# Graph attention layers on one core: value projections moved five slots back, weights and first slots in another order

## Chip, cores and metric

One core of a Trainium2 chip. The metric is the device time of one execution in microseconds; lower is better.

## What is computed

128 graphs of 128 nodes with 512 features, one adjacency matrix `adj` for all. Two layers, each behind a layer norm without weights (`h` is always the normalised, rectified x):

```python
h = relu(layernorm(x));  a = adj @ h              # per graph
x = x + relu(max_over_features(a) + b0)           # what the reference's first layer comes to
q, k, v = h2 @ Wq + bq, h2 @ Wk + bk, h2 @ Wv + bv   # 8 heads of 64
x = x + softmax(q k^T / 8, masked by adj == 0) @ v
```

The column added by the first layer is the same for all features of a node, so the second layer norm gives the same h as the first (but for eps); the kernel uses one h for both. `bv` is added to x at the end, as the weights of a softmax sum to 1.

## The kernel before

The work goes by graphs, one slot per graph, with an instruction order written out by hand for each engine and semaphores between them. Products are made at about float32 precision from float16 pairs: each operand is a head (the float16 value) and a rest (what the head lacks), and three matmuls (head x head, head x rest, rest x head) stand for one (PAIRS). Each matrix is scaled by a power of two found from its largest absolute value (`peak_of`, `peak_to_rows` on TensorE, `scales_of`), then `w_head` (ScalarE, L378) and `w_rest` (VectorE, L525) split it.

In a slot k, by engine:

- TensorE: scores of graph k-5 (L660); two chunks of the q/k projection of the group of four graphs that k lies in (L631, 12 matmuls of 512 columns each; chunks 0 to 3 are q, 4 to 7 k); the adjacency product of graph k+4 (L616, three matmuls); the values of graph k (`v_rows`, L643, 12 matmuls); probabilities times values of graph k-6 (`probs_times_v`, L675).
- ScalarE: the head of the values of k-1 (`v_head`, L343), the column c of k, the two normalising passes of k+5 (L324, L325), both q/k outputs (`qk_out`, L336 and L338), both exp passes of k-5 (L353, L355), x + c of k (`add_c`, L373, into `xc`).
- VectorE: the maximum of the adjacency product of k+3 (`adjacency_out`, L434), the rest of the values of k-1 (`v_rest`, L439), the softmax shift of k-5 (L450, L454, L457), the output of k-7 (`attention_out`, L464 to L473), the moments of k+6.
- GpSimd: the rest of h of k+5 (L263), rests of q/k (L280), scales of the norm, the rest of the probabilities (L287), x + bv (`add_bv`, L272).
- SP issues all large DMAs: the load of k+7, the transposes of h of k+5 (L193, into `hT`, two groups of four graphs) and of the probabilities of k-5 (L201), the store of k-7. A chunk with u = 0 waits for the transposes of all four graphs of its group.

PSUM: one bank for the adjacency product, one for the values, two for q/k chunks, two for scores, two for probabilities times values (`o_ps`, one graph at a time). So the values of the next graph wait for `v_evac` of the one before, its adjacency for `a_evac`, its outputs for `y_done`.

Before the slots, the first four graphs are normalised, multiplied by the adjacency and transposed, and the weights come in order q, v, k (`MATRICES`), each in one DMA of 1 MB; the k weights are split within slot 0. After the last slot, `TAIL` works off scores, softmax and outputs of the last five graphs, with three sets of banks for the scores (`TAIL_BANKS`).

## Time and profile before

| | us |
|---|---|
| median of 3 runs | 1354.16 (1354.02 to 1355.4) |
| the profiled execution: its time | 1353.57 |
| its span (first to last instruction) | 1351.7 |
| TensorE busy with matmuls | 1298.4 (96%) |
| VectorE busy | 1069.5 (79%) |
| ScalarE busy | 943.1 (70%) |
| GpSimd busy | 1103.6 (82%) |

The span is divided by the timeline into a start, 123 like slots, and an end. A busy share says how much an engine had to do on average, not what set the end; the chain of waits does that. Matmuls that follow each other overlap in the records, so their pace is read from start to start. TensorE's granted clock has two levels here, 1.2 and 2.4 GHz (0.50 and 1.00 in a window).

### The profile page before, as it was taken

How to read it: one execution, taken by the hardware profiler on the slowest of the kernel's cores; microseconds unless marked ns; L12 is line 12 of the kernel's file. 1: busy time of each engine (PE TensorE's matmuls, PEld its weight loads, DVE VectorE, ACT ScalarE, POOL GpSimd, SP SyncE). 2: the span in 40 equal slices, each digit the busy share in tenths (PEclk: the TensorE clock that was granted, in tenths of full speed). 3: DMA queues.
4: the chain of work that ended last, by engine and by line, in shares of the span. 5: the costliest groups of instructions: out<-in, count | busy, mean ns of one | idle time of the engine just before them, and what ended most of it. 6: DMA issues, size and time to landing. Idle time of an engine off the chain costs nothing.

```text
span 1351.7 us, 30371 instructions
## 1 busy us (share of the span) xinstructions
PE 1298.4 (96%) x11145; PEld 681.7 (50%) x11145; DVE 1069.5 (79%) x2229; ACT 943.1 (70%) x1422; POOL 1103.6 (82%) x1160
## 2 busy tenths in 40 slices
PE   4899999999999999999999999999999999999983
PEld 1345555555555555555555555555555555555542
DVE  6458788788887887878878878878788788788777
ACT  4667777777677677677777776777767777767552
POOL 2678898898888888888888888898888898888652
PEclk9999999999999999999999999999999999999995
DMA  7245566565565565665665656656656566566445
GB/s 204 48 91 123 132 133 135 124 141 134 120 141 132 127 138 128 133 141 120 135 138 126 134 132 133 135 127 137 136 119 141 132 133 132 128 140 126 93 73 132
DMA packets 441491, 173.22 MB, mean 128 GB/s; under 512 B 406784, under 2 KB 406912, under 8 KB 441344
## 3 DMA queue, kind: packets, MB, share of 16 engines
q1 hardware_dynamic: 440000, 171.03, 58.0%
q8 instruction: 88, 1.44, 0.4%
q14 instruction: 59, 0.48, 0.1%
q10 hardware_dynamic: 1344, 0.27, 0.1%
HBM read 37.03 MB, written 33.55 MB: 52 GB/s over the span
## 4 chain that ended last, share of the span: by engine, by line
PE 94%; DVE 2%; ACT 0%; DMA 0%; issue 0%; POOLq 0%; ACTq 0%; DVEq 0%
PE proj L631 49%; PE proj L643 24%; PE sc L660 7%; PE o_ps L675 7%; PE proj L616 6%; DVE y L473 1%; DVE masked L450 0%; DVE row_max L454 0%; DVE shifted L457 0%; DMA probsT<-probs 0%; DVE w L525 0%; POOLq L38 0%; ACT qkT L336 0%; ACT qk L338 0%; DVE out_scale L467 0%
## 5 line engine op out<-in xcount | busy, mean ns | idle before, releaser
L631 PE MATMUL proj<-hT,w 128*128 128x512 f16 x3072 | 688.5, 381 | 9.5 <-DMA hT<-h 5.1
L631 PEld LDWEIGHTS proj<-hT,w 128*128 128x128 f16 x3072 | 291.0, 98 | 358.7 <-issue 14.8
L643 PE MATMUL proj<-w,hT 128*128 128x512 f16 x1536 | 352.4, 379 | 1.1 <-DVE w L525 1.1
L336 ACT ACTIVATE qkT<-proj,bqk_up 128x512 f16<-128x512 f32 x256 | 173.5, 678 | 247.2 <-PE proj L631 247.2
L280 POOL TENSOR_TENSOR qkT<-qk,qkT 128x512 f16<-128x512 f32 x256 | 310.8, 1214 | 29.7 <-ACT qk L338 29.3
L287 POOL TENSOR_TENSOR probs<-probs 128x1024 f16<-128x1024 f32 x128 | 273.1, 2134 | 24.3 <-ACT probs L355 24.3
L263 POOL TENSOR_TENSOR h<-h 128x512 f16<-128x512 f32 x125 | 236.1, 1889 | 11.7 <-ACT h L324 8.3
L643 PEld LDWEIGHTS proj<-w,hT 128*128 128x128 f16 x1536 | 150.2, 98 | 182.5 <-DVE w L525 1.5
L439 DVE SCALAR_TENSOR_TENSOR v<-proj,v 128x512 f16<-128x512 f32 x128 | 88.5, 692 | 190.0 <-ACT v L343 190.0
L473 DVE SCALAR_TENSOR_TENSOR y<-o_ps,out_scale,x 128x64 f32<-128x64 f32 x1024 | 208.3, 277 | 4.6
L457 DVE TENSOR_TENSOR shifted<-masked,row_max 128x1024 f32<-128x1024 f32 x128 | 207.9, 1624 | 4.4
L450 DVE SCALAR_TENSOR_TENSOR masked<-sc,score_scale,mask 128x1024 f32<-128x1024 f32 x125 | 160.4, 1283 | 32.4 <-PE sc L660 32.3
L353 ACT ACTIVATE probs<-shifted 128x1024 f16<-128x1024 f32 x128 | 135.3, 1057 | 67.5 <-DVE shifted L457 65.5
L338 ACT ACTIVATE qk<-proj,bqk_up 128x512 f32<-128x512 f32 x256 | 173.8, 679 | 0.0
L272 POOL TENSOR_TENSOR x<-xc,bv_rows 128x512 f32<-128x512 f32 x128 | 163.1, 1274 | 0.0
L454 DVE TENSOR_REDUCE row_max<-masked 128x8 f32<-128x1024 f32 x128 | 156.2, 1220 | 4.4
L242 POOL TENSOR_TENSOR var_eps<-mean_var,eps 128x1 f32<-128x1 f32 x128 | 24.7, 193 | 141.1 <-DVE mean_var L426 141.1
L675 PEld LDWEIGHTS o_ps<-v,probsT 128*128 128x128 f16 x3072 | 113.8, 99 | 48.8 <-DMA probsT<-probs 15.2
L675 PE MATMUL o_ps<-v,probsT 128*128 128x65 f16 (+1 forms) x3072 | 118.1, 195 | 18.9 <-DMA probsT<-probs 14.5
L355 ACT ACTIVATE probs<-shifted 128x1024 f32<-128x1024 f32 x128 | 133.2, 1041 | 0.0
L343 ACT ACTIVATE v<-proj 128x512 f16<-128x512 f32 x128 | 76.4, 597 | 57.8 <-PE proj L643 57.5
L324 ACT ACTIVATE h<-x_in,h_add,h_mul 128x512 f32<-128x512 f32 x128 | 102.8, 803 | 13.0 <-POOL h_add L252 13.0
(59 smaller groups left out, 999.1 us busy)
## 6 DMA issues: line engine op xcount, KB each, us to landing
x_in<-in_x SPq DMA_DIRECT2D x128, 256.0 KB, 3.5
out_x<-y SPq DMA_DIRECT2D x128, 256.0 KB, 2.3
hT<-h SPq DMA_TRANSPOSE x128, 3.0
probsT<-probs SPq DMA_TRANSPOSE x128, 4.3
w_raw<-in_L_gnn_Wq SPq DMA_DIRECT2D x1, 1024.0 KB, 8.9
w_raw<-in_L_gnn_Wv SPq DMA_DIRECT2D x1, 1024.0 KB, 11.1
w_raw<-in_L_gnn_Wk SPq DMA_DIRECT2D x1, 1024.0 KB, 12.8
bv_rows<-in_L_gnn_bv ACTq DMA_DIRECT2D x1, 256.0 KB, 6.6
```

The source lines that it names most:

```text
L263: pool.tensor_tensor(h16[:, k % 4, 1, :], h32[:, k % 2, :], h16[:, k % 4, 0, :], ALU.subtract).then_inc(h_rest_done, 1)
L272: pool.tensor_tensor(x1[:, k % RING, :], xc[:, k % 2, :], bv_rows[:, :], ALU.add).then_inc(x1_done, 1)
L280: pool.tensor_tensor(qk_place(k, u, 1), qk32[:, u % 2, :], qk_place(k, u, 0), ALU.subtract).then_inc(qk_rest_done, 1)
L287: pool.tensor_tensor(probs16[:, k % 2, 1, :, :], probs[:, :, :], probs16[:, k % 2, 0, :, :], ALU.subtract).then_inc(probs_rest_done, 1)
L336: nc.scalar.activation(qk_place(k, u, 0), place, ACT.Identity, scale=P_SCALE, bias=bias).then_inc(qk_head_done, 1)
L338: nc.scalar.activation(qk32[:, u % 2, :], place, ACT.Identity, scale=P_SCALE, bias=bias).then_inc(qk_evac, 1)
L450: nc.vector.scalar_tensor_tensor(masked[:, :, :], banks[:, :, :].rearrange("p t (h n) -> p (t h) n", n=P), score_scale[:, :], mask8[:, :]. ...
L457: nc.vector.tensor_tensor(shifted[:, :, :], masked[:, :, :], row_max[:, :].unsqueeze(2).to_broadcast([P, H, P]), ALU.subtract).then_inc(sh ...
L473: last = nc.vector.scalar_tensor_tensor(y[:, k % 2, cols], o_view[:, h // 4, h % 4, 0:HD], out_scale[:, h // 4, h % 4:h % 4 + 1], x1[:, k ...
L631: last = nc.tensor.matmul(proj[:, u % 2, :], w16[:, j, s, c, col * P:(col + 1) * P], hT[:, k // GROUP % 2, t, c, :, :].rearrange("p g n -> ...
L643: last = nc.tensor.matmul(proj[:, V_BANK, :], hT[:, k // GROUP % 2, s, c, k % GROUP, :], w16[:, 2, t, c, :], start=(c == 0 and i == 0), st ...
L675: last = nc.tensor.matmul(o_view[:, h // 4, h % 4, 0:w], probsT[:, k % 2, s, h % 2 * 4 + h // 2, :], v16[:, t, k // GROUP % 2, k % GROUP, ...
```

## The change

- The values of graph k are projected in slot k+5 (`V_BEHIND` 5), their head and rest follow one slot later (`V_OUT_BEHIND` 6). For that `hT` holds three groups instead of two; `v16` holds one set of four graphs instead of two, so `v_head` also waits for `o_ready` of k-4.
- In the tail, values of the last five graphs stand between their scores; VectorE takes their rests behind the softmax of the same graph, and the outputs of four graphs come at the end. The score banks there are two sets.
- The q weights come in four DMAs with a maximum of each; the order is q, k, v (v behind the x loads). `w_rest` signals each quarter, and chunks 0 and 4 and the first values wait quarter by quarter.
- The first five slots have orders of their own on ScalarE and GpSimd (`early_slot`); k's weights are split in slot 1, v's in slots 3 and 4; graph 4 is normalised in slot 0. The first four transposes are issued by their own loop with semaphores of their own, the others as before.
- `add_c` writes `x1` itself (waiting for `y_done`), `add_bv` adds bv to it in place, four slots later.

```diff
-V_BEHIND, Y_BEHIND = 1, 7
+V_BEHIND, V_OUT_BEHIND, Y_BEHIND, BV_BEHIND = 5, 6, 7, 4
+HT_GROUPS = 3
...
-        hT = sb("hT", [P, 2, 2, KC, GROUP, P], F16)
+        hT = sb("hT", [P, HT_GROUPS, 2, KC, GROUP, P], F16)
...
-        v16 = sb("v16", [P, 2, 2, GROUP, H, VP], F16)
+        v16 = sb("v16", [P, 2, GROUP, H, VP], F16)
...
-        MATRICES = (3, 0, 2, 1)
+        MATRICES = (3, 0, 1, 2)
         TAIL = [(B, k) for k in range(-ATTN_BEHIND, 0)]
-        TAIL_BANKS = (sc, proj[:, 0:2, :], proj[:, 2:4, :])
...
-            for j, w in ((0, wq), (2, wv), (1, wk)):
-                sp.dma_start(w_raw[:, j, :, :], w.rearrange("(c p) n -> p c n", p=P)).then_inc(w_loaded[j], 16)
+            for c in range(KC):
+                sp.dma_start(w_raw[:, 0, c, :], wq[c * P:(c + 1) * P, :]).then_inc(q_loaded[c], 16)
+            sp.dma_start(w_raw[:, 1, :, :], wk.rearrange("(c p) n -> p c n", p=P)).then_inc(w_loaded[1], 16)
             for k in range(PREP_AHEAD, LOAD_AHEAD):
                 load(0, k)
+            sp.dma_start(w_raw[:, 2, :, :], wv.rearrange("(c p) n -> p c n", p=P)).then_inc(w_loaded[2], 16)
...
-                    wait(sp, qk_ready, 2 * (m - m % GROUP - GROUP))
-                    wait(sp, v_ready, m + 1 - 2 * GROUP)
+                    wait(sp, qk_ready, 2 * (m - m % GROUP - (HT_GROUPS - 1) * GROUP))
+                    wait(sp, v_ready, m + 1 - HT_GROUPS * GROUP)
...
-            for k in range(TURN_AHEAD):
-                transpose(0, k)
+            for k in range(GROUP):
+                sp.wait_ge(h_rest_done, k + 1)
+                sp.dma_start_transpose(group_T(k), h16[:, k, :, :].rearrange("p s n -> p (s n)")).then_inc(hT_first[k], 16)
             for k in range(B):
+                if k == 0:
...
-                transpose_probs(B, k)
-                store(B, k - 2)
-            store(B, -2)
-            store(B, -1)
+            for i in range(ATTN_BEHIND):
+                transpose_probs(B, i - ATTN_BEHIND)
+                if i != 2:
+                    store(B, i - STORE_BEHIND - (i > 2))
+            for k in range(-3, 0):
+                store(B, k)
...
+                    pool.tensor_tensor(x1[:, k % RING, :], x1[:, k % RING, :], bv_rows[:, :], ALU.add).then_inc(x1_done, 1)
 
             def qk_rest(base, k, u):
...
-            for k in range(DVE_RESTS, NORM_AHEAD):
+            for k in range(DVE_RESTS, PREP_AHEAD):
...
-                norm_scales(0, k + 1)
+            norm_scales(0, 4)
+            norm_scales(0, 5)
...
+            def early_slot(base, k):
+                u = 2 * (k % GROUP)
+                qk_rest(base, k, u)
+                if k == 0:
+                    rest(base, 4)
+                rest(base, k + NORM_AHEAD)
+                qk_rest(base, k, u + 1)
+                norm_scales(base, k + MOMENTS_AHEAD)
+                add_bv(base, k - BV_BEHIND)
...
                 probs_rest(base, k - ATTN_BEHIND)
                 qk_rest(base, k, u + 1)
-                add_bv(base, k)
-
-            slots(pool, slot)
+                add_bv(base, k - BV_BEHIND)
+
+            for k in range(ATTN_BEHIND):
...
+                slot(0, k)
+            for k in range(-BV_BEHIND, 0):
+                add_bv(B, k)
             for graph in TAIL:
                 probs_rest(*graph)
 
...
+                    nc.scalar.activation(v16[:, 0, k % GROUP, :, 0:HD],
...
                     act.wait_ge(c_done, m + 1)
-                    wait(act, x1_done, m - 1)
-                    nc.scalar.activation(xc[:, k % 2, :], x_in[:, k % RING, :], ACT.Identity, bias=c_col[:, k % RING, :]).then_inc(xc_done, 1)
-
...
-            normalise(0, 4)
-            w_head(2, 2)
             act.wait_ge(bias_loaded, 64)
...
+            def early_slot(base, k):
+                u = 2 * (k % GROUP)
+                if k == 4:
+                    w_head(2, 3)
+                qk_out(base, k, u)
+                if k == 0:
+                    normalise(base, 4)
+                if k == 1:
+                    w_head(1, 2)
+                qk_out(base, k, u + 1)
+                normalise(base, k + NORM_AHEAD)
+                c_of(base, k)
+                add_c(base, k)
...
-                v_head(base, k - 1)
+                v_head(base, k - V_OUT_BEHIND)
...
+            for k in range(ATTN_BEHIND):
+                early_slot(0, k)
+            for k in range(ATTN_BEHIND, B):
+                slot(0, k)
+            v_head(B, -V_OUT_BEHIND)
+            for k in range(-V_BEHIND, 0):
+                v_head(B, k)
+                exps(B, k)
...
+                    nc.vector.scalar_tensor_tensor(w16[:, j, 1, c, :], w_raw[:, j, c, :], up[:, j:j + 1],
+                                                          w16[:, j, 0, c, :], ALU.mult, ALU.subtract).then_inc(rests_done, 1)
...
+            nc.vector.tensor_scalar(mask8[:, :], adj_sb[:, :], 0.0, -8e9, ALU.is_equal, ALU.mult).then_inc(mask_done, 1)
...
+            q_peak_of(0)
             moments(3)
             first_rest(0)
+            q_peak_of(1)
+            first_rest(1)
...
+            q_peak_of(2)
+            q_peak_of(3)
+            dve.wait_ge(q_peaks_done, KC)
+            dve.wait_ge(floor_done, 2)
+            peak_of(0, q_peaks[:, :])
+            floored(0, 2)
             first_rest(2)
-            adjacency_out(0, 1)
...
             scales_of(1)
             projection_scales(0, 1)
             w_rest(0, 1)
+            adjacency_out(0, 0)
             moments(4)
-            w_peak_of(2, 3)
-            adjacency_out(0, 3)
+            moments(5)
+            w_peak_of(1, 3)
+            for k in range(1, PREP_AHEAD):
+                adjacency_out(0, k)
+            moments(6)
             scales_of(2)
-            projection_scales(2, 2)
...
+            projection_scales(1, 2)
+            w_rest(1, 2)
+            dve.wait_ge(undo_done, 2)
+            nc.vector.tensor_tensor(score_scale[:, :], undo[:, 0:1], undo[:, 1:2], ALU.mult).then_inc(score_scale_done, 1)
+            dve.wait_ge(score_scale_done, 1)
             dve.wait_ge(mask_done, 2)
...
-                if base + k > 0:
+                if k > 0:
                     adjacency_out(base, k + AMAX_AHEAD)
-                v_rest(base, k - V_BEHIND)
+                v_rest(base, k - V_OUT_BEHIND)
                 softmax_shift(base, k - ATTN_BEHIND)
...
+                if k > 0:
+                    stats_of(base, k + MOMENTS_AHEAD)
+                    moments_wait(base, k + MOMENTS_AHEAD)
+                    moments_of(base, k + MOMENTS_AHEAD)
+
+            for k in range(B):
+                slot(0, k)
+                if k == 2:
+                    w_peak_of(2, 4)
+                if k == 3:
+                    scales_of(3)
+                    projection_scales(2, 3)
+                    w_rest(2, 3)
+                    dve.wait_ge(redo_done, 3)
+            v_rest(B, -V_OUT_BEHIND)
             for i, graph in enumerate(TAIL):
...
+                softmax_shift(*graph, TAIL_BANKS[i % 2])
+                if i != 2 and i != 4:
+                    attention_out(B, i - Y_BEHIND - (i > 2))
+                v_rest(*graph)
+            for k in range(-4, 0):
                 attention_out(B, k)
...
-                    wait(pe, a_evac, base + k)
+                    wait(pe, a_evac, 1 if k == PREP_AHEAD else base + k)
...
+                        if k < GROUP and col == 0:
+                            pe.wait_ge(rests_done, 2 + j * KC + c)
...
+                        if base + k == 0:
+                            pe.wait_ge(rests_done, 2 + 2 * KC + c)
                         for i, (s, t) in enumerate(PAIRS):
-                            last = nc.tensor.matmul(proj[:, V_BANK, :], hT[:, k // GROUP % 2, s, c, k % GROUP, :],
+                            last = nc.tensor.matmul(proj[:, V_BANK, :], hT[:, (base + k) // GROUP % HT_GROUPS, s, c, k % GROUP, :],
...
+            peak_to_rows(1)
...
-                if isinstance(base, int) and base + k == 0:
+                if k == 1:
                     peak_to_rows(2)
                 qk_chunk(base, k, u + 1)
                 adjacency(base, k + PREP_AHEAD)
+                if k == 3:
+                    peak_to_rows(3)
+                v_rows(base, k - V_BEHIND)
+                probs_times_v(base, k - OUT_BEHIND)
+
+            for k in range(B):
+                slot(0, k)
+            for i, (base, k) in enumerate(TAIL):
+                if i == 1:
+                    pe.wait_ge(qk_evac, 2 * B)
+                if i > 1:
+                    pe.wait_ge(masked_done, base + k - 1)
+                scores(base, k, TAIL_BANKS[i % 2])
                 v_rows(base, k)
-                probs_times_v(base, k - OUT_BEHIND)
-
-            slots(pe, slot, after_first=lambda: peak_to_rows(3))
-            scores(*TAIL[0])
-            pe.wait_ge(qk_evac, 2 * B)
-            scores(*TAIL[1], TAIL_BANKS[1])
-            pe.wait_ge(v_evac, B)
-            scores(*TAIL[2], TAIL_BANKS[2])
-            probs_times_v(B, -OUT_BEHIND)
-            for i, (base, k) in enumerate(TAIL):
-                if i + 3 < len(TAIL):
-                    pe.wait_ge(masked_done, base + k + 1)
-                    scores(*TAIL[i + 3], TAIL_BANKS[i % 3])
-                probs_times_v(base, k)
+                if i == 1 or i == 3:
+                    probs_times_v(B, i // 2 - OUT_BEHIND)
+            for k in range(-4, 0):
+                probs_times_v(B, k)
```

## Rows read from the trace of the kernel before

**Rows 1.** The page: the span, and the chain that ended last by line.

```profile
span 1351.7 us, 30371 instructions
...
PE proj L631 49%; PE proj L643 24%; PE sc L660 7%; PE o_ps L675 7%; PE proj L616 6%; DVE y L473 1%; DVE masked L450 0%; DVE row_max L454 0%; DVE shifted L457 0%; DMA probsT<-probs 0%; DVE w L525 0%; POOLq L38 0%; ACT qkT L336 0%; ACT qk L338 0%; DVE out_scale L467 0%
```

**Rows 2.** TensorE's timeline, first 100 us: start, length, engine, line, work, [idle before, releaser].

```profile
24.42 4.24 PE L631 MATMUL proj<-hT,w 128*128 128x512 f16 x12 [5.08 <-DMA hT<-h]
...
40.60 7.03 PE L631 MATMUL proj<-hT,w 128*128 128x512 f16 x24 [4.45 <-ACT qk L338]
49.43 0.81 PE L616 MATMUL proj<-h,adjT 128*128 128x512 f16 x3 [1.80 <-DVE a_max L434]
50.07 2.75 PE L643 MATMUL proj<-w,hT 128*128 128x512 f16 x12
52.66 5.34 PE L631 MATMUL proj<-hT,w 128*128 128x512 f16 x24
57.84 0.81 PE L616 MATMUL proj<-h,adjT 128*128 128x512 f16 x3
...
78.01 0.84 PE L660 MATMUL sc<-qkT 64*128 64x128 f16 x24
```

**Rows 3.** TensorE's timeline in the last 44 us.

```profile
1308.49 0.84 PE L660 MATMUL sc<-qkT 64*128 64x128 f16 x24
1309.43 1.52 PE L660 MATMUL proj<-qkT 64*128 64x128 f16 x48
1315.43 1.47 PE L675 MATMUL o_ps<-v,probsT 128*128 128x65 f16 x24 [4.47 <-DVE y L473]
...
1345.58 1.50 PE L675 MATMUL o_ps<-v,probsT 128*128 128x65 f16 x24 [4.29 <-DMA probsT<-probs]
```

**Rows 4.** VectorE's timeline in the last 44 us.

```profile
1308.49 0.69 DVE L439 SCALAR_TENSOR_TENSOR v<-proj,v 128x512 f16<-128x512 f32 x1 [2.60 <-ACT v L343]
1309.45 1.28 DVE L450 SCALAR_TENSOR_TENSOR masked<-sc,score_scale,mask 128x1024 f32<-128x1024 f32 x1 [0.26 <-PE sc L660]
...
1313.16 0.22 DVE L464 TENSOR_SCALAR scaled_sum<-o_ps,redo 128x8 f32<-128x8 f32 x1
...
1315.19 1.28 DVE L450 SCALAR_TENSOR_TENSOR masked<-proj,score_scale,mask 128x1024 f32<-128x1024 f32 x1
...
1335.64 1.23 DVE L457 TENSOR_TENSOR shifted<-masked,row_max 128x1024 f32<-128x1024 f32 x1
...
1347.62 1.63 DVE L473 SCALAR_TENSOR_TENSOR y<-o_ps,out_scale,x 128x64 f32<-128x64 f32 x8
```

**Rows 5.** Timeline of ScalarE, VectorE and GpSimd in the first 45 us.

```profile
18.80 2.56 ACT L378 ACTIVATE w<-w_raw,up 128x512 f16<-128x512 f32 x4 [3.93 <-DVE up L508]
...
19.55 2.74 DVE L525 SCALAR_TENSOR_TENSOR w<-w_raw,up,w 128x512 f16<-128x512 f32 x4 [0.21 <-ACT w L378]
...
25.30 0.80 ACT L325 ACTIVATE h<-x_in,h_add,h_mul 128x512 f16<-128x512 f32 x1
...
26.23 1.15 POOL L263 TENSOR_TENSOR h<-h 128x512 f16<-128x512 f32 x1 [1.68 <-ACT h L325]
...
39.22 0.67 ACT L336 ACTIVATE qkT<-proj,bqk_up 128x512 f16<-128x512 f32 x1
...
42.87 4.66 DVE L525 SCALAR_TENSOR_TENSOR w<-w_raw,up,w 128x512 f16<-128x512 f32 x4 [4.57 <-ACT w L378]
```

**Rows 6.** A window early: PE, PEld, DVE, ACT, POOL busy, granted clock, DMA share, GB/s.

```profile
16.00:18.00 2.00, 0.74 (x3) 0.68 (x4) 1.77 (x3) 0.00 (x0) 0.19 (x1) 1.00 1.09 373
```

**Rows 7.** The page's DMA issues, the transposes of h: count, us to landing.

```profile
hT<-h SPq DMA_TRANSPOSE x128, 3.0
```

**Rows 8.** A window at the end, columns as in rows 6.

```profile
1314.00:1315.00 1.00, 0.00 (x0) 0.00 (x0) 1.00 (x6) 1.00 (x2) 0.00 (x0) 0.65 0.00 0
```

**Rows 9.** Timeline of VectorE and ScalarE in slot 127.

```profile
1304.27 1.63 DVE L473 SCALAR_TENSOR_TENSOR y<-o_ps,out_scale,x 128x64 f32<-128x64 f32 x8
...
1306.94 0.72 ACT L373 ACTIVATE xc<-x_in,c_col 128x512 f32<-128x512 f32 x1
```

More of the change, by code:

```diff
@@ L145, in qk_place, with wait_transposed, group_T @@
             return qkT[:, k // GROUP % 2, part, u // KC, u % KC, :, :].rearrange("p g n -> p (g n)")
-        MATRICES = (3, 0, 2, 1)
+        MATRICES = (3, 0, 1, 2)
         TAIL = [(B, k) for k in range(-ATTN_BEHIND, 0)]
-        TAIL_BANKS = (sc, proj[:, 0:2, :], proj[:, 2:4, :])
-        def wait_transposed(eng, base, k):
-            eng.wait_ge(hT_done[k % GROUP], 4 * (base + k - k % GROUP) + 16)
-        def slots(eng, slot, after_first=None):
-            for k in range(B):
-                slot(0, k)
-                if k == 0 and after_first:
-                    after_first()
+        TAIL_BANKS = (sc, proj[:, 0:2, :])
+        def wait_transposed(eng, k):
+            if k < GROUP:
+                eng.wait_ge(hT_first[k], 16)
+            else:
+                eng.wait_ge(hT_done[k % GROUP], 4 * (k - k % GROUP))
+        def group_T(k):
+            return hT[:, k // GROUP % HT_GROUPS, :, :, k % GROUP, :].rearrange("p s c n -> p (s c) n")
         block = ctx.enter_context(nc.Block())
@@ L342, in v_head @@
                     act.wait_ge(v_ready, base + k + 1)
-                    nc.scalar.activation(v16[:, 0, k // GROUP % 2, k % GROUP, :, 0:HD],
+                    wait(act, o_ready, base + k - GROUP + 1)
+                    nc.scalar.activation(v16[:, 0, k % GROUP, :, 0:HD],
                                          proj[:, V_BANK, :].rearrange("p (h d) -> p h d", d=HD),
@@ L371, in add_c, with w_head @@
                     act.wait_ge(c_done, m + 1)
-                    wait(act, x1_done, m - 1)
-                    nc.scalar.activation(xc[:, k % 2, :], x_in[:, k % RING, :], ACT.Identity, bias=c_col[:, k % RING, :]).then_inc(xc_done, 1)
-            def w_head(j, batch):
+                    wait(act, y_done, m - RING + 1)
+                    nc.scalar.activation(x1[:, k % RING, :], x_in[:, k % RING, :], ACT.Identity, bias=c_col[:, k % RING, :]).then_inc(xc_done, 1)
+            def w_head(j, batch, parts=range(KC)):
                 act.wait_ge(scale_done, batch + 1)
-                for c in range(KC):
+                for c in parts:
                     nc.scalar.activation(w16[:, j, 0, c, :], w_raw[:, j, c, :], ACT.Identity, scale=up[:, j:j + 1]).then_inc(heads_done, 1)
@@ L403, in slot @@
                 add_c(base, k)
-            slots(act, slot, after_first=lambda: w_head(1, 3))
-            v_head(B, -1)
-            for graph in TAIL:
-                exps(*graph)
+            for k in range(ATTN_BEHIND):
+                early_slot(0, k)
+            for k in range(ATTN_BEHIND, B):
+                slot(0, k)
[3 more added lines that the diff above has]
+                exps(B, k)
         @block.vector
@@ L432, in adjacency_out @@
                     wait(dve, c_done, m - RING + 1)
-                    rows = FIRST_BANKS[k] if isinstance(base, int) and m < PREP_AHEAD else proj[:, A_BANK, :]
+                    rows = FIRST_BANKS[k] if m < PREP_AHEAD else proj[:, A_BANK, :]
                     nc.vector.tensor_reduce(a_max[:, k % RING, :], rows, AX.X, ALU.max).then_inc(a_evac, 1)
@@ L623, in qk_chunk @@
                         for i in range(GROUP):
-                            wait_transposed(pe, base, k + i)
-                    if isinstance(base, int) and base == 0 and k < GROUP:
-                        pe.wait_ge(rests_done, 2 if u < KC else 4)
+                            wait_transposed(pe, base + k + i)
                     wait(pe, qk_evac, 2 * (base + k) - 1 + u % 2)
```

61 lines of the change are left out of this document (17 added, 44 removed).

## Prediction

> **What bounds the kernel now.** I read the page first: a span of 1351.7 us, and a chain that ended last of which 93% are five lines of matmuls (49, 24, 7, 7 and 6), most of it projections [rows 1]. So the middle is a question of how much TensorE has to do, and only what it does not do at the two ends can be saved. The timeline of TensorE shows one slot at full pace: start to start 0.64 us for the adjacency, 2.59 for the values, 5.18 for two q/k chunks (50.07 less 49.43, 52.66 less 50.07, 57.84 less 52.66) [rows 2]; scores and probabilities-times-values add about 0.8 each [rows 2, 3]. That is 10.0. From the first scores at 78.01 to those of graph 123 at 1308.49 lie 123 slots [rows 2, 3], 10.004 us each: no idle time in them.
>
> Outside it there is idle time. At the start TensorE waits until 24.42 for the transposed activations, again before 40.60 (4.45) and before 49.43 (1.80) [rows 2]. At the end it is through with its dense work at 1310.95 (1309.43 and 1.52), yet the span ends 40.8 us later. There each graph costs VectorE 3.71 us of softmax (1309.45 to 1313.16) and 2.03 of output (1313.16 to 1315.19) [rows 4], while TensorE has 1.5 us of work per graph.
>
> **The start, part by part.** Values of graphs 0 to 4 leave slots 0 to 4: 5 x 2.59 = 12.95 us less TensorE work ahead of slot 5. They come back at the end; nothing is computed less. If all else stood still, slot 5 would begin at 78.01 - 12.95 = 65.1.
> The q weights in quarters, each with its own maximum: the same bytes and the same comparisons, and the first rest (L525) is ready by 22.29 already now (19.55 and 2.74) [rows 5] while TensorE starts at 24.42 behind the transposes [rows 2]. DMA moved 373 GB/s in the stretch before [rows 6] and the same bytes still stand ahead of the transposes in SP's queue, v's included. Three more issues on SP (well under a us each) lie in that shadow. The first activation rest is put behind one quarter's maximum, about 0.9 us later, also in that shadow. I cost all this at nothing; if the cover is gone the bounds are -1 and +1 us.
> From 24.4 on I lay the slots out by the new order. The first chunk ends at 28.5 (24.42, 4.24, at 0.42 us a matmul), the second at 31.1. Graph 4's adjacency now waits for ScalarE's two outputs of chunk 0 (0.67 each), its two normalising passes (0.8 each, started 0.7 apart) and GpSimd's rest (1.15) [rows 5]: to 32.5, 1.4 us of idle time. Slot 1's chunks, with k's maximum between them, end at 38.5. Its adjacency (graph 5) needs a_evac of graph 4, which VectorE reaches only behind k's rests. k's heads come behind chunk 2's output on ScalarE, about 37.1; the rests follow 0.75 later and take 2.74 alone, but 4.66 where GpSimd worked beside them [rows 5]: 40.6 to 42.5, plus 0.3 for the score scale and 0.7 for the maximum. I take 42.2, 3.6 us of idle time; slot 1 ends at 42.8. Slot 2: 5.2 + 0.65 = 48.6. Slot 3: 54.7 with v's maximum. Slot 4 waits for graph 7's transpose: its normalise stands behind chunk 2,5 (48.0 + 1.35 + 1.5 + 1.15, and 3.0 to land [rows 7]) = 55.0 to 55.3. Its chunks end at 60.4. Graph 8's adjacency waits for graph 7's maximum, queued on VectorE behind v's rests, which follow v's heads from 57.8: 61.3 to 63.2, + 0.7. I take 62.4, slot 5 at **63.1**, against 65.1: 2.0 us gained. Bounds: 61.5, and 67 with both rests slow and one restart at half clock (7.03 us for 24 matmuls instead of 5.34 behind the 4.45 us wait [rows 2]).
> The middle: hT in three groups, v16 in one set of four, x1 written in place, bv added four slots later. TensorE, VectorE, ScalarE and GpSimd have the same instructions per slot, SP the same DMAs. The wait for v's head stands as it did (v of one slot is evicted in the next; L439 at 1308.49 follows it [rows 4]), o_ready of k-3 is old when v_head(k) asks, and SP's wait for v_ready is six slots old. Zero; bounds -0.02 and +0.02 us a slot, as far as 10.004 tells, 2.5 us in all.
> So slot 128 starts at 1308.49 - 12.95 - 2.0 = 1293.5.
>
> **The end.** Times from the start of slot 128. VectorE has 0.65 + 5 x 3.71 + 7 x 2.03 = 33.4 us of work there now in a tail of 43.2 (1351.7 - 1308.49). Five v rests come in place of one: 0.65 each. In order: softmax 123 to 4.7, output 121 to 6.7, v rest 123 to 7.35. TensorE's values of 124 wait for that (one bank): 7.4 to 10.0, then p x v of 122 to 10.9; output 122 to 13.2, v rest 124 to 13.85, softmax 125 to 17.6, v rest 125 (values 13.9 to 16.5, head 0.6) to 18.2, softmax 126 to 21.9, output 123 (values 126 from 18.2, p x v to 21.9) to 24.0, v rest 126 to 24.65, softmax 127 to 28.4. From the end of the last softmax (1336.87) to the last p x v (1345.58) are 8.71 us and from there to the end of the span 6.1 [rows 1, 3, 4]: 28.4 + 8.7 + 6.1 = 43.2 with the last p x v at half clock as now, 42.5 at full, is the earliest end. VectorE in the meantime has v rest 127 and outputs 124 to 126, alternating with p x v in the one o_ps: 29.05 + 3 x 2.03 + 3 x 1.5 = 39.6 where p x v of 127 ended at half clock, 38.0 at full; then 2.13 and 2.45 for the store (1351.7 - 1347.62 - 1.63): 42.6 to 44.3. I take 43.4. GpSimd has four adds of bv ahead of its first rest there: its rests start at 7.2 instead of 6.9, hidden.
> The clock. Now TensorE is idle from 1310.95 and its granted clock falls to the lower of its levels (2.4 to 1.2 GHz) in the slice from 1314 to 1315 (0.65) [rows 8]; scores and p x v then take 1.47 to 1.50 instead of 0.8 to 0.9 [rows 3]. In the new tail the longest gap is 3.2 us (4.2 to 7.4), between the 1.80 that left the clock alone and the 4.45 and 4.47 behind which matmuls were slow [rows 2, 3]; the others are 1 to 2.2. After one fall values 124 would take some 1.8 longer, as 24.42 shows [rows 2]. At somewhat under one chance in two I add 0.8: the tail is 44.2, bounds 42.5 and 46.5.
> The Trainium skill, page TensorE: Matmul & The Clock Gate, section "HAM oscillation", says that a kernel whose bursts of matmuls are parted by waits can be throttled anew in every wait and begin each burst cold. By that rule the whole new tail is cold, which is the first rival below, 1349.1; this trace shows a clock that fell once and stayed down through short bursts, and survived gaps of 1.80 us.
>
> **Sum.** Slot 128 at 1293.5 + 44.2 = 1337.7 us of span: 14.0 less. The profiled execution took 1353.57; less 14.0 is 1339.6. The median of the runs is 0.6 above that execution: **1340.2**.
>
> **Rivals.**
> *The tail runs cold.* Values are then 12 x 0.43 = 5.1 us, on VectorE's way wherever only a softmax lies between two v rests. By the same layout: output 122 to 16.1, softmax 125 to 20.45, v rest 125 to 23.2, softmax 126 to 27.05, output 123 to 31.95, softmax 127 to 36.3, and exp of 127 behind values 127 on ScalarE at 38.3; + 8.7 + 6.1 = 53.1, 8.9 more than I take: 1349.1. For: every burst from 1315 to 1346 was slow. Against: the new gaps are shorter and most of the tail is 512-column matmuls, which got the clock back at 24.42 and at 40.60. Chance 0.10.
> *The start gives back.* Each transition (k's rests, v's rests) now has TensorE waiting for a maximum queued behind four VectorE passes; with GpSimd beside them, 1.9 us more each, and a restart of 1.7 each: slot 5 at 68, 1345.1. For: the k rests at 42.87 took 4.66 [rows 5]. Against: at 57 to 62 GpSimd has little in hand. Chance 0.12.
> *Slower than before.* ScalarE's x1 write (L373, last of its slot) now waits for y of k-8 itself. If it waits, the next value head, and with it the value bank, comes late in each of 123 slots. Above 14.0/123 = 0.11 us a slot the change loses; at 0.15 it is 1358.7. Against: L373 of graph 127 runs at 1306.94, when y of graph 120, one later than needed, is done (1304.27 and 1.63) [rows 9]. Chance 0.03.
> *The shift doesn't do what it says*: the values merely lengthen the tail by their 13 us, which needs VectorE to wait for each; that is the first rival in full and its chance is in those 0.10.
>
> **How the numbers follow.** Forecast 0.75, 0.10, 0.12, 0.03. Low: the good ends, 1308.49 - 12.95 - 3.6 + 42.5 = 1334.4 of span, 1336.9; a little margin for the middle gives 1335.5. High: slot 5 two later than the neutral 65.1, tail 46.5: 1344.0 of span, 1346.5; the cold tail stays outside. Some 0.2% (2.7 us) is what a measurement of this kernel can tell from no change. Faster 0.95; same 0.02, the cold tail and the start together; slower 0.03.
>
> **What would show it.** Right: scores of graph 0 at 61.5 to 65 us; slots of 10.00 until scores of graph 123 near 1293; first q matmul still near 24.4 behind DMA of hT; in the tail value matmuls of 216 ns in bursts about 6 us apart, VectorE busy almost throughout, 43 to 46 us from scores 123 to the end. Wrong: a slot of 10.1, a granted clock of 0.5 through the whole tail, VectorE waiting for value heads, or first q matmuls well before 24 us (then the weights' order did free the transposes, which I hold for no gain).

## The result, and the profile after

| | us |
|---|---|
| before, median of 6 runs | 1354.29 (1354.02 to 1355.4) |
| changed, median of 6 runs | 1349.01 (1347.74 to 1350.94) |
| ratio, 95% interval | 0.996 [0.9948, 0.9973] |
| changed, profiled execution: span | 1349.1 (before 1351.7) |

The change is faster, by 5.3 us (0.4%) and not by the 14.0 forecast; the measured median lies above the range (1335.5 to 1346.5). The page of the changed kernel, its span and the chain that ended last by line, answers to [rows 1]: the same five lines of matmuls bound it, 95% of the chain together where 93% were before.

```profile
span 1349.1 us, 30366 instructions
...
PE proj L686 50%; PE proj L698 25%; PE sc L715 7%; PE o_ps L730 7%; PE proj L671 6%; DVE y L514 1%; DMA w_raw<-in_L_gnn_Wq 1%; DVE w L566 0%; DVE shifted L498 0%; SPq L217 0%; DMA hT<-h 0%; DVE v L480 0%; DVE masked L491 0%; DMA out_x<-y 0%; DVE row_max L495 0%
```

The slots in the middle are as they were: scores of graph 0 at 66.18 and of graph 123 at 1296.85 (below), 123 slots of 10.005 us. What the start and the end did is seen apart:

| us | before | forecast | changed |
|---|---|---|---|
| scores of graph 0 (slot 5) | 78.01 | 63.1 (65.1 if nothing else moved) | 66.18 |
| scores of graph 123 (slot 128) | 1308.49 | 1293.5 | 1296.85 |
| from there to the end of the span | 43.2 | 44.2 | 52.25 |

The profiled execution is the longest of the six (1350.94), so the spans differ by 2.6 us where the medians differ by 5.3. In it 11.6 us were gained until slot 128, and the tail gave 9.05 of them back; of the miss of 11.4 in the profiled spans, 8.05 are in the tail, 3.1 in the start, 0.25 in the slots.

TensorE's timeline in the changed kernel's first 70 us, which answers to [rows 2]:

```profile
24.16 7.09 PE L686 MATMUL proj<-hT,w 128*128 128x512 f16 x24 [5.99 <-DMA hT<-h]
32.79 0.82 PE L671 MATMUL proj<-h,adjT 128*128 128x512 f16 x3 [1.54 <-POOL h L272]
...
42.34 1.44 PE L671 MATMUL proj<-h,adjT 128*128 128x512 f16 x3 [3.33 <-DVE a_max L475]
43.58 7.64 PE L686 MATMUL proj<-hT,w 128*128 128x512 f16 x24
...
58.57 5.34 PE L686 MATMUL proj<-hT,w 128*128 128x512 f16 x24 [0.66 <-ACT qk L362]
65.44 0.81 PE L671 MATMUL proj<-h,adjT 128*128 128x512 f16 x3 [1.53 <-DVE a_max L475]
66.18 0.84 PE L715 MATMUL sc<-qkT 64*128 64x128 f16 x24
```

The first q matmul stands where it stood, behind the transposes. The waits are nearly those laid out (1.54, 3.33, 0.66, 1.53; the forecast had 1.4, 3.6, 0.3 to 0.6, 2.0). The third has another releaser than forecast: I had named graph 7's transpose, and it is ScalarE's output of the chunk before. But behind the 3.33 the adjacency takes 1.24 us (43.58 less 42.34) and not 0.65, and slot 2's 24 matmuls 7.47 (51.05 less 43.58) and not 5.18. The windows there, with the granted clock before the DMA share and GB/s at the end of each line, say why: it falls to 0.50 in the wait and stays there until 48 (0.89 from 48 to 49), some seven microseconds.

```profile
40.00:42.00 2.00, 0.00 (x0) 0.00 (x0) 1.97 (x5) 2.00 (x4) 0.00 (x0) 0.85 0.00 0
42.00:44.00 2.00, 1.66 (x4) 0.58 (x5) 1.16 (x4) 1.49 (x3) 1.02 (x1) 0.50 0.06 12
44.00:46.00 2.00, 2.00 (x6) 0.73 (x5) 1.97 (x4) 0.00 (x0) 1.92 (x4) 0.50 0.34 68
```

The tail of TensorE, answering to [rows 3]:

```profile
1296.85 0.84 PE L715 MATMUL sc<-qkT 64*128 64x128 f16 x24
...
1305.12 5.30 PE L698 MATMUL proj<-w,hT 128*128 128x512 f16 x12 [3.96 <-DVE v L480]
...
1314.35 4.45 PE L698 MATMUL proj<-w,hT 128*128 128x512 f16 x12 [2.04 <-DVE v L480]
...
1320.22 2.76 PE L698 MATMUL proj<-w,hT 128*128 128x512 f16 x12 [0.64 <-DVE v L480]
...
1327.37 4.45 PE L698 MATMUL proj<-w,hT 128*128 128x512 f16 x12 [2.88 <-DVE v L480]
...
1335.36 1.47 PE L730 MATMUL o_ps<-v,probsT 128*128 128x65 f16 x24 [2.80 <-DVE y L514]
```

Two windows at its first wait, answering to [rows 8]:

```profile
1304.00:1305.00 1.00, 0.00 (x0) 0.00 (x0) 1.00 (x5) 0.47 (x1) 1.00 (x2) 0.66 0.00 0
1305.00:1307.00 2.00, 1.88 (x5) 0.74 (x6) 1.97 (x3) 0.00 (x0) 1.86 (x1) 0.50 0.00 0
```

And VectorE's timeline there: the shift of graph 123 (the subtraction of the row maxima, L498), the first pass of output 122, the rest of the values of 125, the shift of 126 (compare [rows 4]):

```profile
1300.39 2.04 DVE L498 TENSOR_TENSOR shifted<-masked,row_max 128x1024 f32<-128x1024 f32 x1
...
1311.57 0.23 DVE L505 TENSOR_SCALAR scaled_sum<-o_ps,redo 128x8 f32<-128x8 f32 x1 [2.80 <-PE o_ps L730]
...
1319.47 0.69 DVE L480 SCALAR_TENSOR_TENSOR v<-proj,v 128x512 f16<-128x512 f32 x1 [1.47 <-ACT v L368]
...
1322.64 2.04 DVE L498 TENSOR_TENSOR shifted<-masked,row_max 128x1024 f32<-128x1024 f32 x1
```

TensorE waits 3.96 us for VectorE's rest of graph 123, comes back at half clock, and its values of 124 take 5.30 us where 2.75 were wanted. Those of 125 and 127 take 4.45: there the granted clock was still 1.00 in the microsecond before the first matmul and fell in the first matmuls behind the wait (0.78 from 1314 to 1315, 0.60 from 1328 to 1329). VectorE, which had let TensorE wait, now waits for it: 1.47 us ahead of the rest of 125, 2.80 ahead of output 122 (1308.76 to 1311.57). Moreover two shifts take 2.04 us, where all five in the tail of the kernel before took 1.22 or 1.23. Beside the first of them GpSimd adds bv:

```profile
1297.62 7.16 POOL L280 TENSOR_TENSOR x<-x,bv_rows 128x512 f32<-128x512 f32 x5
```

### The profile page after: what moved, and what is told of

It reads as the page before. It is cut to its first block, busy times and chain, and to the rows that moved or that the text cites. A ratio compares the mean times of both kernels' runs of the same rounds, so it can differ in the third digit from the quotient of the medians.

```text
span 1349.1 us, 30366 instructions
## 1 busy us (share of the span) xinstructions
PE 1303.0 (97%) x11145; PEld 681.0 (50%) x11145; DVE 1071.2 (79%) x2233; ACT 941.9 (70%) x1422; POOL 1106.4 (82%) x1160
## 4 chain that ended last, share of the span: by engine, by line
PE 94%; DVE 3%; DMA 1%; ACT 1%; issue 0%; SPq 0%; POOL 0%; DVEq 0%; ACTq 0%; POOLq 0%
PE proj L686 50%; PE proj L698 25%; PE sc L715 7%; PE o_ps L730 7%; PE proj L671 6%; DVE y L514 1%; DMA w_raw<-in_L_gnn_Wq 1%; DVE w L566 0%; DVE shifted L498 0%; SPq L217 0%; DMA hT<-h 0%; DVE v L480 0%; DVE masked L491 0%; DMA out_x<-y 0%; DVE row_max L495 0%
## 5 line engine op out<-in xcount | busy, mean ns | idle before, releaser
L698 PE MATMUL proj<-w,hT 128*128 128x512 f16 x1536 | 358.4, 384 | 9.5 <-DVE v L480 9.5
L498 DVE TENSOR_TENSOR shifted<-masked,row_max 128x1024 f32<-128x1024 f32 x128 | 211.5, 1652 | 4.4
L280 POOL TENSOR_TENSOR x<-x,bv_rows 128x512 f32<-128x512 f32 x128 | 163.3, 1277 | 0.0
L495 DVE TENSOR_REDUCE row_max<-masked 128x8 f32<-128x1024 f32 x128 | 156.2, 1220 | 4.4
```

The source lines that it names most:

```text
L280: pool.tensor_tensor(x1[:, k % RING, :], x1[:, k % RING, :], bv_rows[:, :], ALU.add).then_inc(x1_done, 1)
L498: nc.vector.tensor_tensor(shifted[:, :, :], masked[:, :, :], row_max[:, :].unsqueeze(2).to_broadcast([P, H, P]), ALU.subtract).then_inc(sh ...
L698: last = nc.tensor.matmul(proj[:, V_BANK, :], hT[:, (base + k) // GROUP % HT_GROUPS, s, c, k % GROUP, :], w16[:, 2, t, c, :], start=(c == ...
```

## The experiments

Each was made on the changed kernel. Since the median of the kernel before lay at 1354.3 to 1355.1 in the four groups of runs, ratios to it (of the mean times) are compared: the change itself has 0.9960. One execution of each kernel has a trace.

**Is it the clock?** Matmuls were put into TensorE's waits of the tail whose product nobody reads, so that it has work there:

```diff
+            def fill(n, bank):
+                for _ in range(n):
+                    nc.tensor.matmul(bank, w16[:, 0, 0, 0, 0:P], w16[:, 0, 0, 0, :], start=True, stop=True)
...
                 scores(base, k, TAIL_BANKS[i % 2])
+                if i == 0:
+                    pe.wait_ge(a_evac, B)
+                fill((0, 13, 8, 2, 8)[i], proj[:, A_BANK, :])
                 v_rows(base, k)
...
             for k in range(-4, 0):
+                fill({-4: 0, -3: 8, -2: 8, -1: 8}[k], proj[:, A_BANK, :])
                 probs_times_v(B, k)
```

> The changed kernel, with 39 matmuls of 512 columns added after the slots, whose product nobody reads, in the bank of the adjacency product: 13, 8, 2 and 8 ahead of the values of graphs 124 to 127, 8 ahead of each of the last three probabilities times values. Theory A (the tail is long because TensorE's clock falls in its waits, and cold values then hold up VectorE): values of 124 to 127 take 2.6 us each instead of 5.1, 4.3, 2.6 and 4.3, the tail (scores of 123 to the end) falls from 52.3 to 44 to 46 us, the time from 1349.0 to 1341 to 1343. Theory B (the tail is VectorE's own chain of softmax, rests and outputs, the cold matmuls lie beside it): no gain, 1349 to 1351.

Measured: 1344.09 (1340.81 to 1346.79), ratio 0.9919 [0.9905, 0.9932]. In the timeline of TensorE the values are warm throughout (at the full granted clock; cold is the half):

```profile
1300.72 2.98 PE L765 MATMUL proj<-w 128*128 128x512 f16 x13
1304.69 2.76 PE L698 MATMUL proj<-w,hT 128*128 128x512 f16 x12 [0.99 <-DVE v L480]
...
1311.02 2.76 PE L698 MATMUL proj<-w,hT 128*128 128x512 f16 x12 [0.23 <-DVE v L480]
...
1322.75 2.76 PE L698 MATMUL proj<-w,hT 128*128 128x512 f16 x12 [1.32 <-DVE v L480]
```

The tail is 46.1 us (1342.5 - 1296.42), 6.2 less, although 55 matmuls were added (31 ahead of values and 24 ahead of products; the 39 of the expectation is a miscount). One window over the whole tail of the changed kernel (VectorE's busy time is the third of the engines', the granted clock the third number from the end):

```profile
1296.90:1349.10 52.20, 30.55 (x325) 17.29 (x324) 37.84 (x91) 12.66 (x15) 18.48 (x11) 0.73 0.36 96
```

And of the kernel with the filled tail:

```profile
1296.40:1342.50 46.10, 34.93 (x382) 18.48 (x379) 37.88 (x91) 13.02 (x15) 18.56 (x11) 0.98 0.41 109
```

VectorE has the same work in both (37.84 and 37.88), and the mean granted clock is 0.73 against 0.98. Theory B falls, in which the cold matmuls lay beside VectorE's chain: VectorE's waits of 2.80 and twice 1.47 us are gone. The median is 1 us above what theory A gave, and the tail 0.1. The runs are spread over 6 us, and their mean granted clock goes with them: 0.997 in the one of 1340.81, 0.992 in that of 1346.79.

**How much does the first wait do?** Only the first 13 of these matmuls (`(0, 13, 0, 0, 0)`, none at the end).

> The same with only the first 13 added matmuls, in the 4 us wait ahead of the values of graph 124. Theory A: that step gets back 2.5 us and the clock stays up until the next long wait, so a part of the gain: 1345 to 1347. Theory B: 1349.

Measured: 1345.43, ratio 0.9932 [0.9919, 0.9944], tail 47.8 (1343.8 - 1295.96). Values of 124, 125 and 126 are warm, those of 127 behind 3.16 us without work are not, in TensorE's timeline:

```profile
1304.24 2.76 PE L698 MATMUL proj<-w,hT 128*128 128x512 f16 x12 [1.00 <-DVE v L480]
...
1310.58 2.76 PE L698 MATMUL proj<-w,hT 128*128 128x512 f16 x12 [2.07 <-DVE v L480]
...
1322.31 4.45 PE L698 MATMUL proj<-w,hT 128*128 128x512 f16 x12 [3.16 <-DVE v L480]
```

One wait carries the greater part of the tail's loss (4.4 of 6.2 us in the profiles, 3.8 of 5.6 by the ratios): with the values of 124 warm, those of 125 are warm too, although TensorE waits as long for them as it did (2.07 here, 2.04 in the changed kernel). TensorE's waits don't grow by cold passes (2.04, 0.64, 2.88 there; 2.07, 0.77, 3.16 here). What a cold pass adds is its own time, as VectorE, which TensorE waits for next, first has to wait for it.

**Is it work, or only that something is issued?** The same 13 matmuls, one column wide:

```diff
-                    nc.tensor.matmul(bank, w16[:, 0, 0, 0, 0:P], w16[:, 0, 0, 0, :], start=True, stop=True)
+                    nc.tensor.matmul(bank[:, 0:1], w16[:, 0, 0, 0, 0:P], w16[:, 0, 0, 0, 0:1], start=True, stop=True)
```

> As the kernel with only the first 13 added matmuls, but each one column wide instead of 512. Theory A (what holds the clock up is work in the array, not that matmuls are issued): the wait stays idle for practical purposes, the values of 124 take 4.4 to 5.3 us, time 1347.5 to 1349.5. Rival (any instruction on TensorE in the wait does it, or the added matmuls act through something else than the clock): values of 124 in 2.6 to 2.8, time 1345.4.

Measured: 1350.61, ratio 0.996 [0.9946, 0.9973], that of the change to the last digit. TensorE's timeline at the same place:

```profile
1300.85 0.48 PE L765 MATMUL proj<-w 128*128 128x1 f16 x13
1304.81 5.30 PE L698 MATMUL proj<-w,hT 128*128 128x512 f16 x12 [3.49 <-DVE v L480]
```

The same number of instructions, and values of 124 in 5.30 again. So the wide ones act by their work. The median lies 1.1 above the range expected; the spread of this kernel's runs (1348.5 to 1351.6) reaches into it.

**The same in the start.** 14 wide matmuls in the wait of slot 1, into the second bank of `o_ps`:

```diff
                 qk_chunk(base, k, u + 1)
+                if k == 1:
+                    fill(14, o_ps[:, 1, :])
                 adjacency(base, k + PREP_AHEAD)
```

> The changed kernel, with 14 matmuls whose product nobody reads in the 3.3 us in which TensorE waits in slot 1 for the maximum of graph 4 (into the second bank of o_ps). Theory A (the restart at half clock behind that wait cost 0.6 us in the adjacency and 2.3 in the 24 matmuls of slot 2): scores of graph 0 start at 63.3 instead of 66.2, time 1346.1. Rival: what slot 2 gains is lost again in the waits of slot 4 (0.66 for ScalarE, 1.53 for VectorE): scores of graph 0 at 66, 1349.

Measured: 1347.84 (1345.94 to 1347.91), ratio 0.9942 [0.9928, 0.9956]. TensorE's timeline:

```profile
38.92 3.19 PE L765 MATMUL o_ps<-w 128*128 128x512 f16 x14
42.41 0.81 PE L671 MATMUL proj<-h,adjT 128*128 128x512 f16 x3 [0.30 <-DVE a_max L475]
43.05 5.34 PE L686 MATMUL proj<-hT,w 128*128 128x512 f16 x24
...
63.36 0.84 PE L715 MATMUL sc<-qkT 64*128 64x128 f16 x24
```

Slot 5 starts at 63.36, 2.8 earlier, as expected to a tenth, and only 0.3 from the forecast's 63.1. The waits of slot 4 (0.67 and 1.52) stay as long as they were, so nothing is lost there. The median lies between the two times expected (1346.1 and 1349). In the ratio 2.4 us are seen of the gain (0.0018 of 1354), but the two intervals overlap: the spread of the runs hides an effect of this size in the time. The profile shows it (the scores of graph 123 start at 1294.03, 2.8 earlier), the time alone does not.

**The wait itself.** VectorE takes the maxima ahead of the rests of the weights:

```diff
             projection_scales(1, 2)
+            adjacency_out(0, 4)
             w_rest(1, 2)
...
-                if k > 0:
+                if k > 1 and k != 4:
                     adjacency_out(base, k + AMAX_AHEAD)
...
                     projection_scales(2, 3)
+                    adjacency_out(0, 7)
                     w_rest(2, 3)
```

> The changed kernel, with VectorE taking the maxima of graphs 4 and 7 before the rests of the k and of the v weights and not behind them. If the order on VectorE is what made TensorE wait (3.33 us in slot 1, and the cold restart of 2.9 behind it, 1.53 in slot 4): scores of graph 0 at 58.5 to 60, time 1341 to 1343. Rival: rests, heads or transposes, which depend on ScalarE, are late next, and half of it comes back as other waits: 61 to 63.5, 1344 to 1346.5.

Measured: 1343.07, ratio 0.9913 [0.99, 0.9927]. TensorE's timeline in the start:

```profile
38.30 0.81 PE L673 MATMUL proj<-h,adjT 128*128 128x512 f16 x3
...
52.17 5.34 PE L688 MATMUL proj<-hT,w 128*128 128x512 f16 x24 [1.14 <-DMA hT<-h]
...
58.09 0.84 PE L717 MATMUL sc<-qkT 64*128 64x128 f16 x24
```

and, later in the same view:

```profile
87.96 0.89 PE L732 MATMUL o_ps<-v,probsT 128*128 128x65 f16 x24 [1.17 <-DVE y L514]
```

Slot 5 at 58.09, 8.1 earlier: both waits on VectorE are gone and the cold restart with them. In their place come 1.14 us for the transposes of slot 4 (the wait I had named there), and 1.17 in slot 7, where probabilities times values wait for y of the graph before: VectorE is behind after the start. 6.4 us are left by the ratios (0.0047 of 1354), 6.8 in the profile (the scores of graph 123 at 1290.09).

**The other half of the wait: one value bank.** In the tail the adjacency bank is free. Values of 124 and 126 go there, and wait for the rest of two graphs before instead of one:

```diff
+        TAIL_V = {-5: V_BANK, -4: A_BANK, -3: V_BANK, -2: A_BANK, -1: V_BANK}
...
-                v_rows(base, k)
+                if i == 1:
+                    pe.wait_ge(a_evac, B)
+                v_rows(base, k, TAIL_V[k], 1 if i == 0 else 2)
```

(`v_rows`, `v_head` and `v_rest` take the bank as an argument.)

> The changed kernel, with the values of graphs 124 and 126 in the bank of the adjacency product, free by then, so that the values of the next graph no longer wait for VectorE's rest of the one before. Theory A (in the tail VectorE waited for cold values that had themselves waited for VectorE; about 7 us of the tail of 52.3): VectorE's own work is left, the tail is 44.6 to 45.6, the time 1341.5 to 1343. If the clock alone was at fault and not the wait: the values still come late after the gap ahead of them, 1346 to 1349.

Measured: 1345.21, ratio 0.9926 [0.9913, 0.9938], and runs within 1.3 us of each other. TensorE's timeline in the tail:

```profile
1300.94 2.76 PE L699 MATMUL proj<-w,hT 128*128 128x512 f16 x12
...
1311.30 2.76 PE L699 MATMUL proj<-w,hT 128*128 128x512 f16 x12 [0.74 <-DVE v L481]
...
1317.66 4.45 PE L699 MATMUL proj<-w,hT 128*128 128x512 f16 x12
```

The tail is 46.6 us (1343.3 - 1296.69): 5.6 less and not the 7 expected, and the median lies between the two ranges expected, nearer to that of the rival (1346). The tail speaks for theory A: values of 124 (1300.94) follow at once, those of 125 and 126 are warm, and the cold ones of 127 (4.45) no longer hold VectorE up. What is missing are VectorE's long shifts, 2.04 and 2.30 us there as well (1.9 together above 1.22), which I had not put in.

**The long shifts.** GpSimd's last adds of bv go behind the rests of the probabilities:

```diff
-            for k in range(-BV_BEHIND, 0):
-                add_bv(B, k)
             for graph in TAIL:
                 probs_rest(*graph)
+                if graph[1] < -1:
+                    add_bv(B, graph[1] + 1)
```

> The changed kernel, with GpSimd's last four adds of bv each behind a rest of the probabilities and not all ahead of the first. They ran beside VectorE's shift (L498) of graph 123, which took 2.04 us instead of 1.22. If GpSimd's work beside it is the cause, that shift is 1.22 again and the tail 0.8 shorter, unless another pass is hit instead: 1348.2. Rival (the pass is long for another reason): 2.04 stays, 1349.

Measured: 1347.1, ratio 0.994 [0.9928, 0.9953]. The shifts of graphs 123, 124 and 126 in VectorE's timeline, and what GpSimd had in hand beside the last two:

```profile
1300.28 1.23 DVE L498 TENSOR_TENSOR shifted<-masked,row_max 128x1024 f32<-128x1024 f32 x1
...
1306.62 1.50 DVE L498 TENSOR_TENSOR shifted<-masked,row_max 128x1024 f32<-128x1024 f32 x1
...
1318.92 2.31 DVE L498 TENSOR_TENSOR shifted<-masked,row_max 128x1024 f32<-128x1024 f32 x1
```

```profile
1305.77 1.27 POOL L280 TENSOR_TENSOR x<-x,bv_rows 128x512 f32<-128x512 f32 x1
...
1318.02 2.13 POOL L295 TENSOR_TENSOR probs<-probs 128x1024 f16<-128x1024 f32 x1 [3.36 <-ACT probs L380]
```

The shift of graph 123 has 1.23 us again; that of 124 (1.50, in the changed kernel 1.22) has an add beside it now, and that of 126 (2.31, in the changed kernel 2.04) the rest of the probabilities, as it had there. So GpSimd's work beside it is the cause. By how much a shift is longer than 1.22 can be read from the two timelines: by some 0.14 us less than the time from its start to the end of the GpSimd pass in hand. That time is 0.42 for 124 (1307.04 less 1306.62; the shift is 0.28 above 1.22), 1.23 for 126 (1320.15 less 1318.92; 1.09 above), 0.96 for 126 in the changed kernel (0.82 above), and the slots of the middle between 600 and 660 us follow it as well (shifts of 1.27 to 2.15 in the changed kernel). So the added length is that of a wait for the GpSimd pass to end, not that of a pass slowed throughout. TensorE's first wait is 0.8 shorter by it, 3.15. The time is 1.9 less by the medians, but the intervals overlap; what it gained beyond the 0.8 can't be told from where the clock happens to fall, as the next kernel shows.

**The q quarters.** One DMA and one maximum again:

```diff
-            for c in range(KC):
-                sp.dma_start(w_raw[:, 0, c, :], wq[c * P:(c + 1) * P, :]).then_inc(q_loaded[c], 16)
+            sp.dma_start(w_raw[:, 0, :, :], wq.rearrange("(c p) n -> p c n", p=P)).then_inc(w_loaded[0], 16)
...
-            q_peak_of(0)
...
-            peak_of(0, q_peaks[:, :])
-            floored(0, 2)
+            w_peak_of(0, 2)
```

> The changed kernel, with the q weights in one DMA and one maximum again. My theory (the first q matmul waits for the transposes, not for weights): first q matmul at 24.2 to 24.4 as before, time 1349.0 within 0.5. Rival (quarters bring the start forward): 0.5 to 2 us longer.

Measured: 1348.75, ratio 0.9956 [0.9944, 0.9969]. The quarters bring nothing: the first q matmul stands at 24.33, behind the transposes. The profile's chain to it does run through the load of the q weights and their maxima, which stand in VectorE's order ahead of the rest of h of graph 2 (at 14.79 here, 15.22 in the changed kernel). But in the kernel before that rest stood ahead of q's maximum, at 13.46, and the first q matmul at 24.42; which speaks against these passes setting it. What holds up the transposes was not tried. In TensorE's timeline of this kernel the tail, of which not a line was changed, is of interest too:

```profile
24.33 8.02 PE L679 MATMUL proj<-hT,w 128*128 128x512 f16 x24 [6.05 <-DMA hT<-h]
```

and, in the tail:

```profile
1305.00 5.11 PE L691 MATMUL proj<-w,hT 128*128 128x512 f16 x12 [3.96 <-DVE v L479]
...
1313.67 2.76 PE L691 MATMUL proj<-w,hT 128*128 128x512 f16 x12 [2.04 <-DVE v L479]
...
1325.40 2.76 PE L691 MATMUL proj<-w,hT 128*128 128x512 f16 x12 [3.15 <-DVE v L479]
```

Behind the same first wait of 3.96 us values of 124 are cold (5.11), but behind 2.04 and even 3.15 us those of 125 and 127 are warm, which took 4.45 each in the profile of the changed kernel. The tail is 49.0 us there (1345.7 - 1296.73) and not 52.25. The two programs differ in the start alone. So waits of 2 to 3 us can go either way behind the same tail code.

**Together.** The maxima first, the two banks, and 8 added matmuls ahead of each of the last three probabilities times values:

> Both repairs in one: the maxima of graphs 4 and 7 ahead of the weight rests, two value banks in the tail, and 8 matmuls whose product nobody reads ahead of each of the last three probabilities times values. If start and tail are independent, the gains add: 1343.1 for the first, 6 to 7 less for the second, 0 to 1.5 for the clock at the very end: 1335 to 1337.5. If they are not (the tail's gain was the same waiting seen twice): 1340 to 1342.

Measured: 1339.18 (1338.91 to 1340.03), ratio 0.9885 [0.987, 0.99]. The parts alone give 0.9960 - 0.0047 - 0.0034 = 0.9879, which lies in this interval. The median lies between the two ranges expected, but the profile decides between them: the scores of graph 123 start at 1290.64 (1290.09 with the maxima alone) and the tail is 46.5 us (1337.1 - 1290.64; 46.6 with the two banks alone), so start and tail are independent. The added matmuls gave nothing: the eight ahead of graph 126 themselves ran cold (3.60 us) and held it up. The 1335 to 1337.5 took the tail's gain at the 7 us that the two banks alone had not brought.

Then without them, but with bv behind, and with the products of 125 and 127 in the two chunk banks:

```diff
+        o_view2 = proj[:, 0:2, 0:H // 2 * VW].rearrange("p t (h e) -> p t h e", e=VW)
...
             for k in range(-4, 0):
-                probs_times_v(B, k)
+                if k == -3:
+                    pe.wait_ge(masked_done, B - 1)
+                probs_times_v(B, k, o_view2 if k % 2 else o_view, 1 if k == -4 else 2)
```

> Maxima of graphs 4 and 7 first, two value banks, bv adds behind the rests of the probabilities, and for graphs 125 and 127 the probabilities times values in the two banks of the q/k chunks, so that they no longer wait for VectorE's output of the graph before (three idle times of 1.66 us on VectorE at the end). No matmuls added. If VectorE's waits there are on the path: 1.5 less than the 1339.2 of the two repairs together, and 0.8 for bv: 1336 to 1337.5. If the chain softmax 127, exp, rest, transpose bounds the end already: 1338 to 1339.5.

Measured: 1337.82 (1337.58 to 1338.03), ratio 0.9871 [0.9858, 0.9884], 11 us better than the change and 17 better than before. The median lies between the two ranges expected. VectorE's three waits for p x v (probabilities times values) are gone, but in their place y of graph 126 waits 3.63 us for the store of graph 124, which is to free its buffer, in VectorE's timeline:

```profile
1329.38 1.63 DVE L516 SCALAR_TENSOR_TENSOR y<-o_ps,out_scale,x 128x64 f32<-128x64 f32 x8 [3.63 <-DMA out_x<-y]
```

And the timelines of SP and TensorE:

```profile
1325.05 1.65 SPq L208 DMA_TRANSPOSE probsT<-probs  x1
1326.75 6.65 SPq L180 DMA_DIRECT2D out_x<-y  x4
...
1328.75 1.49 PE L734 MATMUL proj<-v,probsT 128*128 128x65 f16 x24 [3.79 <-DMA probsT<-probs]
```

y of 124 was done at 1323.35 (1321.72 and 1.63), but SP issues its store only at 1326.75, as the program has that store behind the transposes of the probabilities of 127. So the wait is one for SP's order; another order was not tried. The other path of the expectation lies right behind it: p x v of 127 waits 3.79 us for these transposes and ends at 1330.24, and y of 126 at 1331.01.

## Why the prediction was wrong

- *The middle and the first matmul*: right. 10.005 us a slot; 24.16 behind the transposes; the quarters are worth nothing (one_q). That the q maxima lie in a shadow holds for the time, though the profile's chain runs through them.
- *The start*: its waits were right within 0.5 us each (one of them by another releaser), and slot 5 came 3.1 later than forecast. The step that failed is "Slot 2: 5.2 + 0.65": behind a wait of 3.33 us I let TensorE go on at full clock and kept the restart for the bound. It cost 2.9 us (0.6 in the adjacency, 2.3 in slot 2); with work in the wait slot 5 comes at 63.36.
- *The tail*: the order of work was right, the step that failed is "At somewhat under one chance in two I add 0.8". The clock fell, and more than once: 6.2 us in the profiles (52.25 against 46.1 with work in the waits), 5.6 by the ratios. I had weighed the first wait by itself at 3.2 us. It was 3.96, as the first shift took 2.04 and not 1.22. One fall was put at 1.8 us, after the burst at 24.42; this one cost 2.9 (from start to start the values of 124 took 5.10 and the product behind them 1.24, against 2.60 and 0.83 with the filled wait). And I had counted one fall: the clock fell again at the values of 125 and 127 and at the last products. VectorE waited for the values, a sign of being wrong that the prediction names. The first rival has this mechanism and gave 53.1 us for a tail all cold; it was 52.25, with the values of 126 and all scores warm. It had one chance in ten. That its time, 1349.1, is the measured median is luck: it has neither the 3.1 us of the start nor the long shifts.
- *The rule of the Trainium skill* (TensorE: Matmul & The Clock Gate, "HAM oscillation") spoke for that rival, and the trace after agrees in kind, though not for every burst: values at 5.30, 4.45, 2.76 and 4.45 us, a clock that came back within a burst and fell again behind the next wait. I set it aside on waits of 1.80 us, which prove nothing for one of 3.
- *Shifts beside GpSimd*: not in the sum at all; 0.8 us each, two in the tail. With the waits filled the tail is still 46.1 and not the 43.4 forecast ahead of the term for the clock; 1.9 of these 2.7 us are its two long shifts (2.03 and 2.31). I wrote that GpSimd's adds were hidden, as I looked at who waits for them and not at what runs beside them.
- *"Slower" by ScalarE's wait for y*: not seen; that bound was sound.

What stays open: why the shift (L498) waits for GpSimd's pass and the passes ahead of it don't. It reads two tiles in SBUF (`masked`, `row_max`), L495 one; that this is the difference was not tried. What decides in one run whether a wait of 2 to 3 us costs the clock isn't settled either.

## What to carry to other kernels

Work moved from a dense middle into a tail of waits has to be priced at the clock that the tail will have: between TensorE's levels the same 12 matmuls cost 2.6 or 5.1 us, and where another engine waits for them the difference comes back in every round that is cold. First ask what TensorE waits for (here one value bank, and maxima queued behind weight rests); two lines of order, for two waits, took 6.4 us where filler in the longer of these waits took 2.4, and a second bank took about what the filler of the whole tail did (4.6 and 5.6 us by the ratios, whose intervals overlap), with runs that lie closer together. When a layout has a wait near those that made the engine cold before, forecast both ways instead of shading a mean.

## What was not expected of the hardware

- 13 matmuls whose result is thrown away, in a wait of 4 us, make a kernel 3.6 us faster (1349.01 to 1345.43, 3.8 by the ratios); 13 of one column do nothing (1350.61).
- Runs of one program differ, and their mean granted clock with them: six runs of the changed kernel differ by 3.2 us (mean granted clock 0.985 in the longest, 0.988 in the shortest), five of the one with the filled tail by 6.0 (0.992 and 0.997), of the one with one q load by 4.2 (0.987 and 0.992). With two value banks it is 1.3, and 0.5 in the last kernel. But it is 1.2 too with the maxima first, whose tail is unchanged, so that the tail makes the spread is likely and not shown: in which waits the clock fell is known of the one profiled execution of each.
- VectorE's subtraction of the row maxima (128 x 1024 f32, L498) takes 1.22 us alone. If GpSimd has a float32 pass in hand when it starts, it is longer by what is left of that pass less some 0.14 us (up to 2.31 us in these tails). GpSimd is held up in turn: the add of bv that starts at 1320.11, beside the shift of 2.31, takes 2.25 us instead of 1.27. The pass before the shift (L495) keeps its 1.22 in both cases.
